# Mixture-of-experts loop of a vision tower: 64-row groups on the array, and results in a ring of four that GpSimd copies

## The reference, cut to what matters

```python
def _L1_ffn_ref(x, Wg, bg, We, be, W1, b1, W2, b2):      # D=192, M=768, G=4, E=8, KG=2, KE=4
    xf = x.reshape(-1, D)
    ggates, gidx = _topk_gates(xf @ Wg + bg, KG)
    gw = jnp.einsum('nk,nkg->ng', ggates, jax.nn.one_hot(gidx, G, dtype=xf.dtype))
    egates, eidx = _topk_gates(jnp.einsum('nd,gde->nge', xf, We) + be, KE)
    ew = jnp.einsum('ngk,ngke->nge', egates, jax.nn.one_hot(eidx, E, dtype=xf.dtype))
    combine = gw[:, :, None] * ew
    y = jnp.zeros_like(xf)
    for g in range(G):
        h = jax.nn.gelu(jnp.einsum('nd,edm->enm', xf, W1[g]) + b1[g][:, None, :], approximate=False)
        o = jnp.einsum('enm,emd->end', h, W2[g]) + b2[g][:, None, :]
        y = y + jnp.einsum('end,ne->nd', o, combine[:, g, :])
    return y.reshape(orig_shape)
...
h = h + _L1_ffn_ref(_layernorm(h, axis=-1), ...)
```

## Time and profile before

| | us |
|---|---|
| median of 3 runs | 752.56 (750.7 to 757.16) |
| the profiled execution | 756.36 |
| its span, first to last instruction | 754.6 |
| first and last add of a result (line 654), start | 380.7 and 747.2 |
| mean granted TensorE clock over the span | 0.914 |

### The profile page before, as it was taken

How to read it: one execution, slowest core, us unless ns; L and a number is a source line. 1 busy time by engine, 2 the same in 40 slices (tenths; PEclk the granted TensorE clock), 3 DMA queues, 4 the chain that set the end, 5 groups by cost and what they waited for, 6 DMA issues and landing times.

```text
span 754.6 us, 20437 instructions
## 1 busy us (share of the span) xinstructions
PE 679.0 (90%) x6550; PEld 574.3 (76%) x6550; DVE 406.5 (54%) x1222; ACT 239.0 (32%) x686; POOL 304.8 (40%) x288
## 2 busy tenths in 40 slices
PE   6986948898989999876899799999999999999994
PEld 4754735655755797753799699999999999999994
DVE  6645572845489688878544234444444444444442
ACT  3322312123238311115143233333333333333331
POOL 0111820011023636302354455555655555656554
PEclk9996959587999999975699899999999999999998
DMA  9910000000000003041258454465546566565422
GB/s 325 266 41 2 2 3 2 3 1 3 1 1 0 2 1 120 8 162 50 52 151 234 113 140 127 121 171 113 129 106 178 147 172 171 117 173 126 97 46 39
DMA packets 36136, 70.07 MB, mean 93 GB/s; under 512 B 6481, under 2 KB 21362, under 8 KB 36082
## 3 DMA queue, kind: packets, MB, share of 16 engines
q0 software_dynamic: 15840, 17.71, 13.9%
q10 hardware_dynamic: 8064, 33.12, 12.8%
q1 hardware_dynamic: 12178, 18.48, 7.9%
HBM read 59.31 MB, written 9.98 MB: 92 GB/s over the span
## 4 chain that ended last, share of the span: by engine, by line
PE 72%; DVE 17%; issue 4%; DMA 3%; ACT 1%; POOL 1%; DVEq 0%; ACTq 0%; POOLq 0%; SPq 0%
PE bank L1617 20%; PE bank L1609 14%; PE bank L1612 9%; PE bank L1435 4%; PE bank L1589 4%; PE bank L1367 4%; PE bank L1299 3%; DMA out_dram<-arena,number_u 2%; PE bank L1387 2%; DVE stats L941 1%; DVE zx L955 1%; PE bank L1378 1%; DVE arena L1175 1%; DVE arena L1172 1%; PE bank L1405 1%
## 5 line engine op out<-in xcount | busy, mean ns | idle before, releaser
L654 POOL DMA_INDIRECT out_dram<-arena,number_u x80 | 126.8, 1585 | 54.9 <-DMA out_dram<-arena,number_u 28.1
L648 POOL DMA_INDIRECT arena<-normed_rows,fetch_u x80 | 78.4, 980 | 113.8 <-DMA out_dram<-arena,number_u 42.1
L841 ACT ACTIVATE arena<-bank,arena 128x128 f32<-128x128 f32 x234 | 64.6, 375 | 120.9 <-PE bank L1612 116.9
L1260 DVE COPY arena<-bank 128x256 f32<-128x256 f32 x81 | 34.4, 425 | 118.4 <-PE bank L1589 109.8
L1617 PE MATMUL bank<-arena 128*128 128x192 f32 x468 | 83.4, 327 | 0.7 <-ACT arena L841 0.7
L1617 PEld LDWEIGHTS bank<-arena 128*128 128x128 f32 x468 | 76.0, 191 | 1.0 <-ACT arena L841 1.0
L1279 DVE TENSOR_SCALAR arena<-bank,arena 128x192 f32 x80 | 33.4, 418 | 62.2 <-PE bank L1617 60.6
L1609 PE MATMUL bank<-arena 128*128 128x128 f32 x468 | 60.1, 279 | 4.3 <-DVE arena L1260 4.3
L1609 PEld LDWEIGHTS bank<-arena 128*128 128x128 f32 x468 | 58.3, 195 | 5.1 <-DVE arena L1260 5.1
L551 POOL TENSOR_SCALAR rstd<-mv 128x4 f32<-128x4 f32 (+1 forms) x15 | 3.6, 237 | 143.5 <-DVE mv L944 143.5
L841 ACT ACTIVATE arena<-bank,w_space 128x128 f32<-128x128 f32 x132 | 36.4, 375 | 68.6 <-PE bank L1612 68.6
(11 more groups left out here) (259 smaller groups left out, 1235.0 us busy)
## 6 DMA issues: line engine op xcount, KB each, us to landing
arena<-in_moe_w_dram ACTq DMA_DIRECT2D x14, 579.0 KB, 5.7
arena<-in_moe_w_dram ACTq DMA_DIRECT2D x14, 576.0 KB, 4.3
arena<-in_xf_dram SPq DMA_DIRECT2D x16, 256.0 KB, 10.6
w_space<-in_moe_w_dram ACTq DMA_DIRECT2D x7, 579.0 KB, 5.4
w2small<-in_moe_w_dram ACTq DMA_DIRECT2D x7, 579.0 KB, 5.7
w_space<-in_moe_w_dram ACTq DMA_DIRECT2D x7, 576.0 KB, 3.8
wab<-in_moe_w_dram ACTq DMA_DIRECT2D x7, 576.0 KB, 4.1
arena<-in_w_dram SPq DMA_DIRECT2D x8, 480.0 KB, 7.4
```

What stands on the lines that cost most here:

```text
L648: pool.indirect_dma_start(out=mo_stage[:, s * ROWN:(s + 1) * ROWN], out_offset=None, in_=normed_rows, in_offset=bass.IndirectOffsetOnAxis( ...
L654: pool.indirect_dma_start(out=out, out_offset=bass.IndirectOffsetOnAxis(ap=number_u[:, s:s + 1], axis=0), in_=mo_res[:, s * D:(s + 1) * D] ...
L841: nc.scalar.activation(mo_hT[:, m, :], bank[2 + m][:, 0:P], ACT.Gelu, bias=b1[:, m:m + 1]).then_inc(free[2 + m], 1)
L1260: nc.vector.tensor_copy(mo_xT.rearrange("p k t -> p (k t)"), bank[1][:, 0:2 * P]).then_inc(free[1], 1)
```

## The change

What it does, engine by engine:

- First layer: the 192 features are cut in three chunks of 64 (`CHUNKS`). All 18 matmuls per tile contract 64 rows, in pairs: hidden chunk n in rows 0 to 63 of the array and chunk n+3 in rows 64 to 127 run on the same 64 features. For this the transposed rows stand twice in `mo_xT`, in partitions 0 to 63 and again in 64 to 127, and the weights are laid out anew on the host (same bytes).
- Second layer: each of the six chunks is contracted in two halves of 64 rows, one into bank 0 and one into bank 1, so 12 matmuls. VectorE scales bank 0 into `mo_new` and adds the scaled bank 1 to it.
- Transposes: six of 64 tokens each, in two row groups, into columns 128 to 319 of banks 2 and 5. They stand ahead of the second layer as before. The wait for the staged rows and for banks 2 and 5 stands ahead of the last pair of the first layer.
- ScalarE takes the hidden chunks in the order 0, 3, 1, 4, 2, 5.
- Results: `mo_new` is a ring of four (`RESULTS`). VectorE no longer copies to `mo_res` and no longer copies the token numbers. GpSimd copies both, in its own queue: the numbers ahead of the fetch, the result ahead of the add; its add waits for its copy. `result_free` now counts GpSimd's copies and starts at four.
- One bank of the table step ahead of the loop is another one (7 for 5).

```diff
+CHUNKS = D // 64
+HIDDEN_DONE = tuple(m + half for m in range(MC // 2) for half in (0, MC // 2))
+COLUMNS_AT, COLUMN_BANKS = P, (2, 2 + MC // 2)
+RESULTS = 4
-W1N = HID + MC // 2 * P
+W1N = MC // 2 * CHUNKS * P
...
+            pool.sem_inc(sem("result_free"), RESULTS)
             with pool.Fori(0, pairs) as pair:
                 for s in range(2):
                     i = pair * 2 + s
...
+                    tile, new = pool.snap(i + 0), pool.snap(i % RESULTS * D)
                     pool.wait_ge(sem(f"accumulated{s}"), added)
-                    pool.sem_inc(sem("result_free"), 1)
+                    nc.gpsimd.tensor_copy(number_u[:, s:s + 1], table_u[:, bass.ds(tile, 1)])
                     pool.wait_ge(sem("fetch_set"), fetch_set)
...
                     pool.wait_ge(sem("result_ready"), result)
+                    pool.sem_inc(sem("adding"), 1)
+                    nc.gpsimd.tensor_copy(mo_res[:, s * D:(s + 1) * D], mo_new[:, bass.ds(new, D)]).then_inc(sem("result_free"), 1)
+                    pool.wait_ge(sem("result_free"), pool.snap(i + (RESULTS + 1)))
                     pool.sem_inc(sem("adding"), 1)
                     pool.wait_ge(sem(f"accumulated{1 - s}"), settled)
...
             def stage_rows(i):
                 dve.wait_ge(sem("rows_in"), i * 16 + 16)
-                dve.wait_ge(full[1], i + moe_base[1])
+                if not isinstance(i, int) or i:
+                    dve.wait_ge(sem("columns_full"), i)
...
-                nc.vector.tensor_copy(mo_x[:, D:2 * P], mo_stage[:, bass.ds(i % STAGE * ROWN + P, REST)])
-                nc.vector.tensor_copy(mo_x[:, 0:D], mo_stage[:, bass.ds(i % STAGE * ROWN, D)]).then_inc(sem("rows_staged"), 1)
+                for half in range(2):
+                    ins = nc.vector.tensor_copy(mo_x.rearrange("p (k h x) -> p k h x", k=CHUNKS, h=2)[:, :, half, :], mo_stage[:, bass.ds(i % STAGE * ROWN, D)].rearrange("p (k x) -> p k x", k=CHUNKS))
+                ins.then_inc(sem("rows_staged"), 1)
...
             def take_columns(i):
-                dve.wait_ge(full[1], i + (moe_base[1] + 1))
-                nc.vector.tensor_copy(mo_xT.rearrange("p k t -> p (k t)"), bank[1][:, 0:2 * P]).then_inc(free[1], 1)
+                dve.wait_ge(sem("columns_full"), i + 1)
+                for r, b in zip((0, REST), COLUMN_BANKS):
+                    ins = nc.vector.tensor_copy(mo_xT[:, :, r:r + REST], bank[b][:, COLUMNS_AT:COLUMNS_AT + D].rearrange("p (k t) -> p k t", k=CHUNKS))
+                ins.then_inc(sem("columns_taken"), 1)
...
-                    nc.vector.tensor_copy(number_u[:, bass.ds(half, 1)], table_u[:, bass.ds(tile, 1)])
-                    dve.wait_ge(free[0], summing)
-                    nc.vector.tensor_copy(mo_res[:, bass.ds(to, D)], mo_new[:, bass.ds(new, D)]).then_inc(sem("result_ready"), 1)
+                    dve.wait_ge(full[0], low)
+                    ts(out=mo_new[:, bass.ds(new, D)], in0=bank[0][:, 0:D], scalar1=mo_gates[:, bass.ds(gate, 1)], scalar2=None, op0=ALU.mult).then_inc(free[0], 1)
+                    dve.wait_ge(full[1], high)
+                    dve.wait_ge(free[0], low)
+                    stt(out=mo_new[:, bass.ds(new, D)], in0=bank[1][:, 0:D], scalar=mo_gates[:, bass.ds(gate, 1)], in1=mo_new[:, bass.ds(new, D)], op0=ALU.mult, op1=ALU.add).then_inc(free[1], 1)
+                    dve.wait_ge(free[1], high)
+                    dve.sem_inc(sem("result_ready"), 1)
...
                 with pe.Fori(first, end) as i:
-                    pe.wait_ge(free[1], i + (moe_base[1] + 1))
-                    for m in range(MC):
-                        mm(bank[2 + m][:, 0:P], w1e[:, m * P:(m + 1) * P], mo_xT[:, 0, :], start=True, stop=False)
-                    for m in range(MC):
-                        r, c = m % 2 * REST, HID + m // 2 * P
-                        mm(bank[2 + m][:, 0:P], w1e[r:r + REST, c:c + P], mo_xT[r:r + REST, 1, :], start=False, stop=True).then_inc(full[2 + m], 1)
-                    transpose_rows(i + 1)
+                    pe.wait_ge(sem("columns_taken"), i + 1)
+                    for n in range(MC // 2):
+                        for k in range(CHUNKS):
+                            c = (n * CHUNKS + k) * P
+                            if n * CHUNKS + k == MC // 2 * CHUNKS - 1:
+                                pe.wait_ge(sem("rows_staged"), i + 2)
+                                for b in COLUMN_BANKS:
+                                    pe.wait_ge(free[b], i + (moe_base[b] + 1))
+                            for r, m in ((0, n), (REST, n + MC // 2)):
+                                ins = mm(bank[2 + m][:, 0:P], w1e[r:r + REST, c:c + P], mo_xT[r:r + REST, k, :], start=(k == 0), stop=(k == CHUNKS - 1))
+                                if k == CHUNKS - 1:
+                                    ins.then_inc(full[2 + m], 1)
+                    transpose_rows()
                     pe.wait_ge(free[0], i + moe_base[0])
-                    for m in range(MC):
+                    pe.wait_ge(free[1], i + moe_base[1])
+                    for n, m in enumerate(HIDDEN_DONE):
                         pe.wait_ge(free[2 + m], i + (moe_base[2 + m] + 1))
-                        ins = mm(bank[0][:, 0:D], mo_hT[:, m, :], w2e[:, m, :], start=(m == 0), stop=(m == MC - 1))
-                    ins.then_inc(full[0], 1)
+                        for r, b in ((0, 0), (REST, 1)):
+                            ins = mm(bank[b][:, 0:D], mo_hT[r:r + REST, m, :], w2e[r:r + REST, m, :], start=(n == 0), stop=(n == MC - 1))
+                            if n == MC - 1:
+                                ins.then_inc(full[b], 1)
```

More of the change, by code:

```diff
@@ L291, in vit_tower @@
         mo_gates = view(P, 4 * NE)
[L292 to L293 removed]
+        mo_x = view(P, CHUNKS * P)
+        mo_xT = view(P, CHUNKS * P).rearrange("p (k t) -> p k t", k=CHUNKS)
         mo_res = view(P, 2 * D)
[L295 removed]
+        mo_new = view(P, RESULTS * D)
         mo_w1 = [w1_space[:, 0:W1N], wab[:, 0:W1N]] + [view(P, W1N) for _ in range(2)]
@@ L401, in plan @@
                 use(0, "table", 0)
-                use(5, "table", 1)
+                use(7, "table", 1)
             elif step == "cT":
@@ L831, in expert @@
                 if e and e + AHEAD - 1 < NE:
-                    act.wait_ge(full[0], first + moe_base[0])
+                    act.wait_ge(full[1], first + moe_base[1])
                     load_expert(act, (u + AHEAD - 1) % AHEAD, e + AHEAD - 1)
@@ L837, in expert @@
                 with act.Fori(first, end) as i:
-                    act.wait_ge(full[0], i + moe_base[0])
-                    for m in range(MC):
+                    act.wait_ge(full[1], i + moe_base[1])
+                    for m in HIDDEN_DONE:
                         act.wait_ge(full[2 + m], i + (moe_base[2 + m] + 1))
@@ L1272, in _ @@
                     stage_rows(i + 2)
-                    gate, to = dve.snap(i % 4 * NE + e), dve.snap(i % 2 * D)
-                    new = dve.snap(i % 4 * D)
-                    added, summing = dve.snap(i + 1), dve.snap(i + (moe_base[0] + 1))
-                    half, tile, ahead = dve.snap(i % 2), dve.snap(i + 0), dve.snap(i + 4)
+                    gate, new = dve.snap(i % 4 * NE + e), dve.snap(i % RESULTS * D)
+                    added, low, high = dve.snap(i + 1), dve.snap(i + (moe_base[0] + 1)), dve.snap(i + (moe_base[1] + 1))
+                    half, ahead = dve.snap(i % 2), dve.snap(i + 4)
                     nc.vector.tensor_copy(fetch_u[:, bass.ds(half, 1)], table_u[:, bass.ds(ahead, 1)]).then_inc(sem("fetch_set"), 1)
-                    dve.wait_ge(full[0], summing)
-                    ts(out=mo_new[:, bass.ds(new, D)], in0=bank[0][:, 0:D], scalar1=mo_gates[:, bass.ds(gate, 1)], scalar2=None, op0=ALU.mult).then_inc(free[0], 1)
-                    dve.sem_inc(sem("scaling"), 1)
                     dve.wait_ge(sem("result_free"), added)
                     dve.sem_inc(sem("scaling"), 1)
-                    nc.vector.tensor_copy(number_u[:, bass.ds(half, 1)], table_u[:, bass.ds(tile, 1)])
-                    dve.wait_ge(free[0], summing)
-                    nc.vector.tensor_copy(mo_res[:, bass.ds(to, D)], mo_new[:, bass.ds(new, D)]).then_inc(sem("result_ready"), 1)
+                    dve.wait_ge(full[0], low)
[5 more added lines that the diff above has]
+                    dve.sem_inc(sem("result_ready"), 1)
         @block.tensor
```

24 lines of the change are left out of this document (11 added, 13 removed).

## The result

The changed kernel takes 782.83 us (median of 5 runs, 780.57 to 789.54) where the kernel before takes 752.56: ratio 1.0416, interval 1.0367 to 1.0465, slower by 30 us. The forecast was 770, the range 737 to 798.

The account below looks back on a forecast made before the run. TensorE bounds the kernel now (4.53 us per tile); changed, GpSimd would at 4.4. 79 x 4.4 + 36 of late landings = 383.6 for 366.5, plus 0.4 at the start: +17.5 us, 752.56 to 770; range 737 to 798.

Parts of the forecast that it names:

- GpSimd becomes the bound: GpSimd's string of add, copies and fetch: 4.4 us per tile where TensorE needs 4.2.
- The 3.60: Shortest distance between GpSimd's adds before the change, read as its fastest, leaving 0.9 us per tile for late landings.
- Late landings can't be made good: Late DMA landings on GpSimd's fetches and adds, made good before, now add 36 us in the loop.
- Left 36: Late landings in GpSimd's loop: at most 48.6 us, less 11 to 12 of cover, leaves 36.
- 11 to 12 us of cover: Deducted from late landings: GpSimd's copies cover 0.4 us of the add's wait on each of 28 experts with a load.
- rival 2: GpSimd is the bound but late landings mostly hide in its longer cycle: 745 to 760 us, chance 0.2.
- VectorE costs nothing on the path: VectorE's 0.6 us more work per tile is covered by its 2.2 us of idling: nothing on the path.
- TensorE's tile 4.2: TensorE's tile in the expert loop falls from 4.53 to 4.2 us, 26 us in the loop if nothing else holds it.
- ScalarE: nothing: ScalarE's new Gelus order and a load waiting for bank 1, one instruction later, cost nothing.
- Rival 1: TensorE keeps the pace and late landings are taken up: 718 to 728 us, half true 738; faster, chance 0.2.
- Rival 4: TensorE waits for rows long enough to lose its clock, a tile taking up to 8.4 us: slower, chance 0.08.
- The rule of the Trainium skill that was left out of the sum: VectorE holding up GpSimd's copy through shared SBUF interfaces by 0.26 us per tile: cycle 4.66, 20 us more, 790.

Follow-up runs that it names:

- e1: Changed kernel, but VectorE copies the result and token numbers again and GpSimd's queue is as before: 753.67 us, ratio 0.9997.
- e2: Kernel before plus only the ring of four and both copies in GpSimd's queue, TensorE as before: 790.31 us, ratio 1.0453.
- e8: Changed kernel with GpSimd's copy of the result made twice, the first into an array nothing reads: 802.65 us, ratio 1.0577.
- e3: Changed kernel without weight loads in the expert loop, all experts using the first four's weights: 744.69 us.
- e5: e1 without weight loads in the expert loop, the same weights for all as in e3: 735.74 us, ratio 0.9725.
- e12: Changed kernel with two semaphores for the rows, so a fetch waits for the fetch two before it: 763.96 us, ratio 1.0126.
- e7: e6 with VectorE's expert loop written out 32 times, one bound read per change of expert instead of two: 748.67 us, ratio 0.99.
- e9: e7 with the weight loads of the expert loop issued by SyncE in place of ScalarE: 743.93 us, ratio 0.9873.
- e11: e9 with the fetch ahead of the wait for an old add, and two row semaphores so two fetches may be under way: 733.48 us, ratio 0.973.
- e6: Changed kernel with GpSimd's loop written out for four tiles, no copies on GpSimd, none of a result on VectorE: 746.96 us, ratio 0.9877.

## Why the prediction was right, point by point

- **GpSimd becomes the bound: right, and shown.** e1 takes its copies away and the loss goes, e2 has nothing but them and has the whole loss, e8 adds one and every cycle grows. The cycle was taken as 4.4 us, the sum gave 4.41; it is 4.34 (4.28 and 4.38 in turn). The 3.60 that was read as GpSimd's fastest distance before is not: 25 of the 79 are shorter, down to 3.17, so the room was up to 1.36 us per tile and not 0.9. The longer cycle by itself costs little, 9 us (e3 against e5): the adds of e5, with GpSimd's old queue and no loads, are 4.37 apart in the mean, no less than GpSimd's new 4.34. The copy was 0.36 for 0.34, from its end to the add 0.94 to 1.06 for 0.94. The copy of numbers with its gaps was taken as 0.187 and two gaps; it shows 0.19 beyond the add and one gap of 0.17, since it begins while the add's record still runs.
- **Late landings can't be made good: right in kind, the term mis-sized.** The step "Left 36" is the one that is off. In the profiled execution the 398.9 us are 79 x 4.34 = 342.9 and 56.0 beyond it, for 36 in the sum. That the forecast's 383.6 is short by 15 and not by 20 is luck: its cycle was 0.06 us too long, 4.7 in 79 distances, and covers so much of the missing landings. Of the 56, 9.3 are there without loads too (e3), at most 3.8 of them by the next point; by the medians the loads cost 38 (e3 against the changed kernel). The 11 to 12 us of cover that had been deducted were not tested by themselves. How a landing gets on the string most stands in the prediction only as a word against rival 2, without a price: through the fetch that waits for the fetch before it. It is 44.5 us in 21 waits, and 19 us of time come back when two fetches may be under way (e12).
- **VectorE costs nothing on the path: wrong at a change of expert.** Its cover was reckoned tile by tile, from the mean idle time of 2.2 us (of the 180 us, 170 wait for TensorE). At a change it reads two loop bounds (2.3 us), and with 0.6 us more work and a tile 0.34 shorter the columns come 0.3 too late: 0.47 us at each change. In e5 that is 13 us (the tile distances are 16.1 above 79 x 4.19, of which 3.2 in the first two tiles), in e3, where GpSimd's 4.34 covers a part, at most 3.8. The experiment that reads one bound less, e7, did not bring it as time.
- **TensorE's tile 4.2: right (4.19).** The low end of its sum is 4.13 by its own terms (2.01 + 1.95 + 0.17), not 4.16. TensorE's waits for rows came in 18 tiles, not in most of them. That this was worth 26 us "if nothing else holds TensorE" is the condition that failed, with or without GpSimd's copies: e1 gains nothing.
- **ScalarE: nothing.** Right for the sum, wrong as a statement on the loop: at 4.19 us its issuing of loads, 0.8 us and more in front of the Gelus, is on the path (e7, e9). At 4.53 it was covered but for one tile of 5.55 us, in whose middle the issue took 1.95.
- **Rival 1** (718 to 728) was priced by GpSimd's low ends alone. e1 has GpSimd's old queue, and stands at 753.67: its chance of 0.2 looks high in hindsight, since e5 to e11 found more limits within 0.3 us of TensorE's new tile. **Rival 2** is refuted by e3: the loads do not hide.
- **Rival 4**, the clock, came in small, and the mean over the span (0.912, before 0.914) hides it. Behind the first tile of the loop the granted clock is at the lower level, 0.50, in one stretch before (427.21 to 434.04), and in four of 3.4 us after (from 457.52, 491.65, 546.27 and 716.93). Each of the four begins 0.6 to 1.3 us after TensorE had waited 1.3 to 1.8 us for rows, waits of the size that the prediction gives as the reason for its 0.08; behind waits of 1.37 to 1.49 us elsewhere (to 627.63, 638.81 and 704.31) the clock stayed at 1.00. One of the four, in TensorE's timeline and in the busy time of the stretch (columns as in the earlier trace rows):

```profile
545.39 0.49 PE L1632 MATMUL bank<-arena 64*128 64x128 f32 x4 [1.81 <-DVE arena L1266]
545.71 0.35 PE L1603 MATMUL bank<-ident,arena 64*128 64x64 f32 x6
546.56 3.74 PE L1641 MATMUL bank<-arena 64*128 64x192 f32 x24 [0.50 <-issue]
...
546.27:549.68 3.41, 3.12 (x20) 3.15 (x22) 1.62 (x7) 0.26 (x2) 2.37 (x3) 0.50 0.22 41
```

  The four second layers take 3.4 to 3.7 us from start to start in place of 2.00, 6.4 us in all. It did not make the kernel slower by the rival's way: the distances of the adds that begin in these stretches are 4.38, 4.87, 4.38 and 4.44, and the next ones 4.28 to 4.38.
- The rule of the Trainium skill that was left out of the sum, 790 with it (GPSIMD Engine Reference, Key points: GpSimd shares its SBUF interfaces with VectorE), did not add to the cycle. All 80 copies of a result take 343 to 358 ns, so none was held up by 0.26:

```profile
L658 POOL COPY arena<-arena x80: 343/355/358, 380.6 to 779.3; 128x192 f32 x80
```

  But this hardly tests the rule: 32 of them had no VectorE instruction beside them, 44 only such as read PSUM, and the four with a VectorE copy within SBUF took 347 to 356. On VectorE's side the trace of the kernel before agrees with the reading of the earlier trace rows: the 36 result copies with no GpSimd instruction beside them take 259 to 261 ns, and all nine above 300 run beside a fetch or an add.

- **Open:** in e11 two tiles of 8.69 and 9.41 us remain, 10 of its 17.5 us above 79 x 4.19. In them TensorE waits 2.48 and 1.94 us for rows whose fetch landed late, and the granted clock is 0.50 from 426.01 for 3.4 us and from 634.23 for 6.8. Why these fetches are late is open; around the first wait (421.60 to 426.00) the DMA engines are 18% busy, so the traffic of a load is not all of it. Why e7 gains nothing over e6 while 16 more of its tiles run at TensorE's pace is settled in part only: its VectorE waits 35.8 us for rows where e6 has 8.5, and its profiled execution has two stretches at a clock of 0.50 behind the first tile (tiles of 8.34 and 8.26 us) where that of e6 has none. No run of the changed kernel moved its wait for an old add behind the fetch.

## What to carry to other kernels

An engine that is idle nearly half of the time can hold the slack that the kernel lives on: compare its shortest cycle, not its busy share, with the bound's, and ask what makes late transfers good after the change. When the bound's stage gets shorter by 0.3 us, look for every step that had less cover than that at the irregular places (a change of loop, a tile with a load), not in the mean tile. A queue in which each transfer waits for the one before it passes every delay on; a semaphore for each buffer was worth 7 and 19 us here.

## Not expected of the hardware

GpSimd's adds take 1607 ns and its fetches 1003 to 1005 in every kernel in which it also copies (the changed one, e2, e3, e8, e12), and 1583 to 1585 and 980 to 981 in those in which it doesn't (before, e1, e9, e11). A copy of one number per partition, 183 and 184 ns where GpSimd stood idle before it, has a record of 767 ns when it is queued behind an add, beginning 1.04 us into it, and ends 0.2 us after it. Two copies of 128 x 192 in a row have records of 0.35 us each but begin 0.29 apart.
